# ScalarE multiplies the rows of both norms by their inverse root mean square; TensorE broadcasts the first modulation rows; the orders of work laid anew

## What is computed

```python
mod = (silu(c) @ wmod).reshape(8, 6, 1, 128)
sa, ca, ga, sb, cb, gb = mod[:, 0], ..., mod[:, 5]      # ga, gb: kept at least 0.25 away from 0
h = layernorm(x) * (1 + ca) + sa
x = x + ga * attn(h)       # h * rsqrt(mean(h*h) + eps) * w; in_proj; causal conv; silu;
                           # softplus; state-space recurrence of 4 heads; gate by silu(z); out_proj;
                           # and h itself is added as the residual
h = layernorm(x) * (1 + cb) + sb
x = x + gb * ffn(h)        # soft MoE: h / |h| * sqrt(128) * gamma; logits against 512 normed slots;
                           # softmax over tokens and over slots; 8 experts; combine
```

## Time and profile before

| | us |
|---|---|
| median of 3 runs (256.5 to 257.06) | 257.02 |
| the profiled execution, its own time | 258.02 |
| its span, first to last instruction | 256.3 |
| busy: PE, DVE, ACT, POOL | 215.7, 150.1, 130.5, 48.3 |
| granted TensorE clock, mean | 0.993 |

### The profile page before, as it was taken

The page is one execution under the profiler, slowest core; times in us unless marked ns, Lnnn a source line. Parts: engine busy times, 40 slices in busy tenths (PEclk is TensorE's granted clock), DMA queues, the critical chain, the costliest instruction groups (busy, mean ns, idle before and its releaser), DMA issues.

```text
span 256.3 us, 3390 instructions
## 1 busy us (share of the span) xinstructions
PE 215.7 (84%) x1141; PEld 136.9 (53%) x1141; DVE 150.1 (59%) x463; ACT 130.5 (51%) x270; POOL 48.3 (19%) x91
## 2 busy tenths in 40 slices
PE   3611998799778977989899789987999999998895
PEld 0311555655545756637566548674444445454894
DVE  2786788599889998679698786561020110102353
ACT  2444239964055676559932247556827254360460
POOL 5126920001462477000001640000000000000000
PEclk9999999999999999999999889999999999999999
DMA  7360000020032000000410000000033230500022
GB/s 197 79 205 1 1 0 0 12 76 0 5 128 77 0 3 0 4 0 0 132 39 0 0 1 3 0 3 0 0 82 82 51 113 0 164 4 0 20 64 82
DMA packets 13488, 10.42 MB, mean 41 GB/s; under 512 B 1582, under 2 KB 11287, under 8 KB 13471
## 3 DMA queue, kind: packets, MB, share of 16 engines
q1 hardware_dynamic: 10982, 9.02, 11.8%
q10 hardware_dynamic: 2488, 1.19, 1.9%
HBM read 9.08 MB, written 1.07 MB: 40 GB/s over the span
## 4 chain that ended last, share of the span: by engine, by line
PE 54%; DVE 25%; ACT 8%; POOL 4%; issue 4%; DMA 3%; ACTq 2%; DVEq 0%; POOLq 0%
PE bank L511 49%; DVE xcT L1205 3%; DVE cmax L1303 2%; DVE rmax L1294 2%; POOL root L463 2%; DVE bst L1054 2%; DVE hh L1136 2%; DMA rsm<-ksm 2%; ACT xcT L905 2%; DMA out_dram<-xin 1%; DVE BT L1318 1%; DVE hh L1128 1%; DVE xntok L1159 1%; PE bank L808 1%; PE bank L759 1%
## 5 line engine op out<-in xcount | busy, mean ns | idle before, releaser
L1340 DVE SCALAR_TENSOR_TENSOR seg_e<-bank,vecT,gbT 128x512 f32<-128x512 f32 x8 | 6.0, 751 | 54.1 <-PE bank L511 54.1
L511 PE MATMUL bank<-slotsT,w_sb 128*128 128x512 f32 x64 | 28.2, 593 | 0.8 <-issue 0.8
L511 PE MATMUL bank<-eo,xhT 128*128 128x129 f32 (+1 forms) x192 | 24.1, 283 | 4.4 <-DVE xhT L1277 3.3
L511 PE MATMUL bank<-xnT,winT 128*128 128x512 f32 x48 | 25.7, 666 | 1.7 <-ACT BT L908 1.7
L511 PEld LDWEIGHTS bank<-eo,xhT 128*128 128x128 f32 x192 | 22.8, 195 | 5.9 <-DVE xhT L1277 3.7
L995 ACT ACTIVATE zsT<-bank,vecT 128x512 f32<-128x512 f32 x16 | 11.0, 688 | 21.0 <-PE bank L511 20.9
L511 PEld LDWEIGHTS bank<-slotsT,w_sb 128*128 128x128 f32 x64 | 12.1, 190 | 15.9 <-issue 14.1
L463 POOL TENSOR_TENSOR root<-root,neg_half 128x2 f32<-128x2 f32 (+1 forms) x24 | 20.1, 837 | 2.0
L458 POOL TENSOR_SCALAR root<-mv 128x2 f32<-128x2 f32 (+1 forms) x12 | 4.1, 346 | 86.2 <-DVE mv L1057 81.8
L1205 DVE SCALAR_TENSOR_TENSOR xcT<-bank,convw,xcT 128x510 f32<-128x510 f32 (+2 forms) x24 | 17.7, 738 | 4.2 <-ACT xcT L905 4.2
L1268 DVE TENSOR_TENSOR seg_m<-seg_e,gm 128x512 f32<-128x512 f32 x24 | 15.5, 686 | 5.6 <-ACT seg_e L945 5.6
(11 more groups left out here) (164 smaller groups left out, 401.9 us busy)
## 6 DMA issues: line engine op xcount, KB each, us to landing
w_sb<-in_L_ffn_w_dram SPq DMA_DIRECT2D x16, 256.0 KB, 3.0
mods_bc<-mod_dram SPq DMA_DIRECT2D x8, 320.0 KB, 3.9
xin<-in_L_attn_x_dram SPq DMA_DIRECT2D x4, 256.0 KB, 3.6
out_dram<-xin SPq DMA_DIRECT2D x8, 128.0 KB, 1.8
eo<-in_L_wmod_dram ACTq DMA_DIRECT2D x1, 384.0 KB, 3.4
eo<-in_L_attn_in_proj_w_dram ACTq DMA_DIRECT2D x1, 384.0 KB
eo<-n_L_ffn_slot_embeds_dram ACTq DMA_DIRECT2D x1, 256.0 KB, 3.4
eo<-n_L_attn_out_proj_w_dram ACTq DMA_DIRECT2D x1, 128.0 KB
```

Of the source, the lines that this page charges most:

```text
L511: return nc.tensor.matmul(o, lhsT, rhs, start=start, stop=stop)
L1340: V.scalar_tensor_tensor(eoT[:, :, j, :], bank[4 + j][:, :].rearrange("p (b s) -> p b s", b=B), vecT[:, bass.ds(it * 2 + (RB2 + j), 1)], g ...
```

## The change

- `unit1` and `unit2` become visits of ACT: an Identity activation with the root as a scale of its own for each partition, in place of DVE's multiplication. Sixteen tiles for each of the two norms in all.
- The shift and scale rows of sublayer one of the first pass no longer go through HBM. PE multiplies `cs` of one batch, broadcast over 128 columns, by the first 256 columns of `wmod`, so that a PSUM bank has the rows on all partitions, and adds the 1 with a matmul of ones. `centre1` and `modulate1` of pass 0 read the bank (`mod_of`). The other rows go through HBM as before, later; `mods_bc` of pass 0 is loaded without its first two rows. POOL's `add_basis` now waits for them. The 1 is added to all scales on PE.
- Of `wmod`, ACT loads 256 columns first, SP the rest later. Input weights, small vectors and the row `dt_nat` are loaded by SP, in the order c, x of unit 0, input weights, x of unit 1, rest of `wmod`, vectors, small ones.
- `s_ready` is gone. What was the preamble's tail becomes single visits (`once`) in the lists: on ACT `scale_win`, `unit_slots`, `small_rows`, `copy_wo`, `copy_sn` and the second `rsm_rows`, most of which DVE did before; on DVE `vectors`, `rows_of_mods`, `gate_columns`; on PE `t_wo`, `t_slot_embeds`; on POOL `slot_roots`.
- `UNIT_AT` is gone. A visit has four whole numbers, one for each unit and pass, its turn on its engine; so the two passes have orders of their own.

```diff
-        UNIT_AT = [0.0, 4.04, 91.03, 95.07]
...
-        def pipeline(eng, visits):
+        def pipeline(eng, visits, once=()):
 
-            todo = sorted((p + UNIT_AT[j + 2 * it], n, j, it) for n, (p, _) in enumerate(visits)
-                          for it in range(PASSES) for j in range(2))
+            todo = sorted([(turns[j + 2 * it], n, j, it) for n, (turns, _) in enumerate(visits)
+                           for it in range(PASSES) for j in range(2)]
+                          + [(turn, n, None, None) for n, (turn, _) in enumerate(once)])
...
-            mm(bank[5][0:B, 0:3 * P], cs[:, :], wmod_sb[:, 0:3 * P])
-            mm(bank[6][0:B, 0:3 * P], cs[:, :], wmod_sb[:, 3 * P:6 * P])
-            mm(bank[7][:, 0:B], wmod_sb[:, tile_cols(5)], cs[:, :]).then_inc(s_pe0, 1)
+            one_row = ident[:, 0:1].broadcast_to((P, P))
+            for j in range(2):
+                for bi in range(BP):
+                    b, o = j * BP + bi, bank[5 + j][:, 2 * bi * P:2 * (bi + 1) * P]
+                    mm(o, cs[:, b:b + 1].broadcast_to((P, P)), wmod_sb[:, 0:2 * P], stop=False)
+                    q = mm(o[:, P:2 * P], ones_sq[:, :], one_row, start=False)
+                q.then_inc(s_pe0, 1)
             pe.wait_ge(s_vec, N_VEC)
-            nc.tensor.transpose(bank[0][:, 0:VR], vec_nat[:, :], ident[0:VR, 0:VR])
-            pe.wait_ge(s_w, N_W)
+            nc.tensor.transpose(bank[0][:, 0:VR], vec_nat[:, :], ident[0:VR, 0:VR]).then_inc(s_pe0, 1)
+            pe.wait_ge(s_w, 16)
...
+            def unit1(j, it):
+
+                wait(act, root_done, j, it, 2)
+                for t in range(TP):
+                    q = A(xntok[j][:, t, 0:P], hh[j][:, t, :], ACT.Identity, scale=root[j][:, t:t + 1])
+                q.then_inc(xn_done[1][j], 1)
+
+            def unit2(bi):
+                def visit(j, it):
+                    wait(act, ms_root_done, j, it, bi + 1)
+                    for t in range(bi * NT, (bi + 1) * NT):
+                        q = A(xn2tok[j][:, t, 0:P], hh[j][:, t, :], ACT.Identity, scale=root[j][:, t:t + 1])
+                    q.then_inc(xn2_done[1][j], 1)
                 return visit
...
-            pipeline(act, visits)
+            pipeline(act, visits, once=[(3, scale_win), (5, unit_slots), (6, small_rows), (9, copy_wo), (12, copy_sn),
+                                        (13, lambda: rsm_rows(1).then_inc(s_act0, 1))])
...
+            def vectors():
+
+                dve.wait_ge(s_pe0, PE_VEC)
+                step0(V.tensor_copy(vecT[:, :], bank[0][:, 0:VR]))
+                assert n0[0] == DVE_VEC
+                step0(V.tensor_tensor(g_all[:, :], vecT[:, RG:RG + 1], vecT[:, RSG:RSG + 1], ALU.mult))
+                assert n0[0] == DVE_G
...
+            def mod_of(j, it, bi, m):
+
+                if it == 0 and m < 2:
+                    return bank[5 + j][:, (2 * bi + m) * P:(2 * bi + m + 1) * P]
+                return mods_bc[j][:, bi, m, :]
...
             def centre1(j, it):
-                wait(dve, mods_in, j, it)
+                if it:
+                    wait(dve, mods_in, j, it)
+                else:
+                    dve.wait_ge(s_pe0, PE_MOD[j])
                 wait(dve, var_done, j, it)
                 centre(j, it, 0, range(BP), own_norm1)
...
-            pipeline(dve, visits)
+            pipeline(dve, visits, once=[(0, vectors), (7, rows_of_mods), (8, gate_columns)])
```

One line of the new numbers, of ACT's list (unit1 and unit2, for j, it = 0,0; 1,0; 0,1; 1,1):

```diff
+                      ((64, 66, 122, 123), exps(1)), ((68, 74, 124, 125), copy_slotsT(1)), ((2, 10, 65, 69), unit1),
+                      ((44, 48, 103, 108), unit2(0)), ((46, 52, 106, 112), unit2(1))]
```

More of the change, by code:

```diff
@@ L529, in _ @@
[L529 to L536 removed]
+            pe.wait_ge(s_wo, N_WO)
+            nc.tensor.transpose(bank[2][:, 2 * P:2 * P + H], dt_nat[:, :], ident[0:H, 0:H]).then_inc(s_pe0, 1)
@@ new lines, in _, with t_wo @@
+            pe.wait_ge(s_wmod_b, 16)
+            mm(bank[7][0:B, 0:3 * P], cs[:, :], wmod_sb[:, 0:3 * P], stop=False)
+            mm(bank[7][0:B, P:2 * P], ones_sq[:, 0:B], one_row, start=False)
+            mm(bank[4][0:B, 0:3 * P], cs[:, :], wmod_sb[:, 3 * P:6 * P], stop=False)
+            mm(bank[4][0:B, P:2 * P], ones_sq[:, 0:B], one_row, start=False)
+            mm(bank[7][:, 3 * P:3 * P + B], wmod_sb[:, tile_cols(5)], cs[:, :]).then_inc(s_pe0, 1)
+            def t_wo():
+                pe.wait_ge(s_dve0, DVE_ROWS)
+                for k in range(CT):
+                    q = nc.tensor.transpose(bank[7][:, tile_cols(k)], wo_nat[:, tile_cols(k)], ident[:, :])
+                q.then_inc(s_pe0, 1)
@@ L538, in _, with t_slot_embeds @@
+            def t_slot_embeds():
+                pe.wait_ge(s_act0, ACT_SE_UNIT)
+                for m in range(MT):
+                    q = nc.tensor.transpose(bank[4][:, tile_cols(m)], se_nat[:, m, :], ident[:, :])
+                q.then_inc(s_pe0, 1)
             pe.wait_ge(s_pool, POOL_ALL)
-            pe.wait_ge(s_ready, 3)
             def t_xn(j, it):
@@ L862, in _, with scale_win, unit_slots, copy_wo @@
                 act.wait_ge(s_act0, ACT_TANH + m + 1)
-            act.wait_ge(s_small, N_SMALL)
-            A(expA_t[:, :], expA_row[:, :], ACT.Exp).then_inc(s_act0, 1)
-            act.wait_ge(s_pool, POOL_ALL)
-            for j in range(2):
-                A(rsm[j][:, :, :], blk[:, 1, :].unsqueeze(2).broadcast_to((P, H, W)), ACT.Copy).then_inc(s_act0, 1)
-            act.wait_ge(s_ready, 1)
+            def scale_win():
+                act.wait_ge(s_dve0, DVE_VEC)
+                act.wait_ge(s_pe0, PE_W)
+                w = vecT[:, RNW:RNW + 1]
+                A(winT[:, 0:512], bank[1][:, :], ACT.Identity, scale=w).then_inc(s_act0, 1)
+                A(winT[:, 512:ROWS], bank[2][:, 0:ROWS - 512], ACT.Identity, scale=w).then_inc(s_act0, 1)
+            def unit_slots():
+                act.wait_ge(s_pool, POOL_SE)
+                for m in range(MT):
+                    q = A(se_nat[:, m, :], se_nat[:, m, :], ACT.Identity, scale=se_r[:, m:m + 1])
+                q.then_inc(s_act0, 1)
+            def copy_wo():
+                act.wait_ge(s_pe0, PE_WO)
+                A(woT[:, :, :], bank[7][:, 0:CT * P].rearrange("p (k d) -> p k d", k=CT), ACT.Copy).then_inc(s_act0, 1)
+            def copy_sn():
+                act.wait_ge(s_dve0, DVE_G)
+                act.wait_ge(s_pe0, PE_SE)
+                A(snT[:, :], bank[4][:, :], ACT.Identity, scale=g_all[:, :]).then_inc(s_act0, 1)
+            def small_rows():
+                act.wait_ge(s_small, N_SMALL)
+                A(expA_t[:, :], expA_row[:, :], ACT.Exp)
+                for k in range(CT):
+                    A(diag_d[:, k, :], ident[:, :], ACT.Identity, scale=d_col[:, k:k + 1])
             def mods(j, it, bi):
@@ L1151, in visit @@
                     wait(dve, var_root_done, j, it, bi + 1)
-                    modulation(j, 1, [bi]).then_inc(h2_done[1][j], 1)
-                return visit
-            def unit1(j, it):
-                wait(dve, root_done, j, it, 2)
-                for t in range(TP):
-                    q = V.tensor_scalar(xntok[j][:, t, 0:P], hh[j][:, t, :], root[j][:, t:t + 1], None, ALU.mult)
-                q.then_inc(xn_done[1][j], 1)
-            def unit2(bi):
-                def visit(j, it):
-                    wait(dve, ms_root_done, j, it, bi + 1)
-                    for t in range(bi * NT, (bi + 1) * NT):
-                        q = V.tensor_scalar(xn2tok[j][:, t, 0:P], hh[j][:, t, :], root[j][:, t:t + 1], None, ALU.mult)
-                    q.then_inc(xn2_done[1][j], 1)
+                    modulation(j, it, 1, [bi]).then_inc(h2_done[1][j], 1)
                 return visit
```

218 lines of the change are left out of this document (111 added, 107 removed).

## The result

| | before | changed |
|---|---|---|
| median (lowest to highest), 20 runs each | 258.71 (256.24 to 261.33) | 259.58 (258.77 to 261.88) |
| ratio, 95% interval | | 1.0058 (1.003 to 1.0086) |
| the profiled execution, its span | 258.02, 256.3 | 261.88, 259.9 |
| granted TensorE clock in it | 0.993 | 0.933 |

The change is slower by 0.6% by the ratio, about 1.5 us (0.9 us by the medians), where 1.7 us less than before were forecast. The 20 runs of the kernel before have a higher median than the three shown ahead of the prediction (257.02 us).

The account below looks back on a forecast made before the run. It took a thin chain to bound the head, then PE, DVE and ACT in turns, DVE in the hand-over, PE in the experts. Terms summed to -1.7 us, forecasting 255.3 us; own range 253.9 to 256.6, whole range 250.9 to 258.2 us.

Parts of the forecast that it names:

- The sum: Whole kernel: five terms, -3.0 + 1.1 - 0.2 + 0.1 + 0.3, give -1.7 us, span 256.3 to 254.6 us.
- The head: Up to the first projection: mods' broadcast by PE starts it earlier, by 2.6 to 3.6 us, taken as 3.0 us.
- ACT while the first projections run: First pass: work moved to ACT exceeds its idle time before unit 1's exponential, costing 1.1 us.
- The hand-over: First to second pass: `token_max` 1.4 us later through ACT's queue, offset by DVE's relief; 0.2 us gained.
- The table loads: Second-pass projections: two more loads of 1.28 us each and the silu nearly fit ACT's idle time; 0.1 us lost.
- The end of the second pass: ACT's queue holds `copy_logits(0)` back about 2.0 us, PE's new order gives it back; 0.3 us lost.
- the second rival: ACT's queue: waits for POOL's roots cost 1.4 and 2.0 us, nothing gives them back; +1.6 us, 258.6 us, chance 0.13.
- The first rival: DVE's relief in hand-over and second norms counts in full, 4.5 us; about 250.7 us, chance 0.22.
- the third rival: The head does not come early: vectors' loads land 2.6 us behind PE and hold every norm; 257.9 us, chance 0.14.
- fourth rivals: The fourth: second-pass table loads meet no idle time on ACT, 3.1 us more; 258.4 us, chance 0.06.

Follow-up runs that it names:

- b: Changed kernel with `unit2` moved back to DVE and `unit1` left on ACT; median 257.09 us, ratio to before 0.9889.
- d: Changed kernel with ACT's copies of xn2T and logits ahead of waiting `unit2` visits, one PE pair swapped; median 257.04 us, ratio to before 0.995.
- h: Changed kernel with unit 0's second-pass silu later on ACT, so two table loads go; median 259.48 us, ratio to before 1.0062.
- i: Changed kernel with SP issuing the six vector loads ahead of projection weights and x of unit 1; median 258.5 us, ratio to before 1.0052.
- c: Changed kernel with DVE's `vectors` moved behind the centring of both units; median 254.94 us, ratio to before 0.9898.
- k: f plus ACT's second `rsm_rows` directly behind the first and `copy_sn` ahead of unit 1's `copy_xnT`; median 251.35 us, ratio to before 0.9774.
- g: Changed kernel with the edits of c and d together; median 252.92 us, ratio to before 0.979.
- e: Changed kernel with `unit1` and `unit2` both moved back to DVE; median 258.35 us, ratio to before 1.0016.
- f: Changed kernel with the edits of b and c together; median 252.27 us, ratio to before 0.9753.
- j: f with PE's broadcast undone, the first pass's mods going through memory again; median 263.09 us, ratio to before 1.0236.
- l: k plus DVE's `unit2(1)` of unit 1 in the first pass one turn earlier; median 251.5 us, ratio to before 0.9786.
- a: Kernel before with only `unit1` and `unit2` moved from DVE to ACT; median 263.0 us, ratio to before 1.0175.

## Why the prediction was wrong

**"The sum": -1.7 us forecast, +1.5 us measured.** The terms in turn.

- **The head, -3.0 us: right as a number, for the changed kernel as built.** Four kernels have its head: b, d, h and i begin P 3.1 to 3.5 us before 25.94 us. The profiled execution itself, with -1.6 us, had the vectors land later. "DVE's `vectors` ahead of the first statistics" was seen, and put down as giving away part of the gain. It was not priced: c shows 4.7 us.
- **ACT while the first projections run, +1.1 us: right as a number, and partly by luck.** P to Y grew by 0.9 to 1.9 us in b, d, h and i, 2.35 us in the profiled execution. ACT was indeed without idle time before unit 1's exponential in b, d and i, at 35.8 to 36.1 us for the 36.2 us forecast. But PE's idle time in P to Y grew by only 0.5 us (2.2 to 2.6 us) in these four. The other 0.4 to 1.4 us are PE at work: four transposes of the slot embeddings that stand there now (0.60 us at 31.01 us in the changed kernel, 0.60 us in h, 1.06 us in i), and pace (the twelve 512-column instructions of unit 1 took 5.49 us in i and 7.19 us in h). In k ACT was idle for 3.11 us before that exponential, and P to Y was 28.77 us all the same, against 28.63 us in c.
- **"The hand-over", -0.2 us: the step that failed.** Y to P' grew by 1.3 us in the profiled execution and by 1.8 us in c, h and i. The text had "1.4 us later" for `token_max`, from ACT's queue, and then let the order and DVE's relief give it all back. Two things were wrong. The delay began at `copy_xn2T`, one step earlier than at `copy_logits`: `unit2(1)` of unit 0 was ahead of that copy in the order, and only unit 1's `unit2` was looked at. So PE stood idle 2.2 us before the logits of c, h and i, for 0.47 us before, and L is 1.9 us later. And the giving back was counted in waits alone. As waits it came: over the whole stretch PE is idle 0.5 to 1.0 us less than before. But its work took 2.2 to 2.5 us longer, of which the first four logits, behind that wait, are 1.7 to 1.8 us (3.63 to 3.78 us for 1.98 us). In the head the prediction priced PE's pace; here it put it at nothing, without a reason. How much of the lower pace the wait brings is not settled: b and d, with 0.47 us of idle time there, had it in this place too, g didn't.
- **The table loads, +0.1 us: right** in that they are hidden (h). P' to Y' is 0.5 us longer, and h does not shorten it; in c, d, e, f, g, i, j and l it is 25.9 to 26.2 us. All of these eight have a granted clock of 0.93 in this stretch; before, changed, a, b, h and k have 1.00.
- **The end of the second pass, +0.3 us: too small, for the same reason.** Y' to X is 50.58 us against 49.71 us in the profiled executions, 0.9 us more, though 49.5 to 49.9 us in c, h and i. The kernel before had a low spell of its own there, a granted clock of 0.94 in Y' to L', and this hid most of the loss. Against b, with the clock at 1.00, the queue costs 1.66 us in Y' to L', and Y' to X is 1.5 to 2.6 us longer. PE's idle time over Y' to X is nearly the same in all kernels of the second table, 5.9 to 6.5 us, so that the order gave the wait back, as was forecast; what is left is the pace behind the wait:

```profile
150.88 3.78 PE L537 MATMUL bank<-snT,CTr 128*128 128x512 f32 x4 [2.23 <-ACT CTr L987]
```

So the second rival, ACT's queue waiting for POOL's roots, came in: 0.13 was its chance, +1.6 us its price, +1.5 us the result. Its condition was stated and held: PE's first `shifts(1)` of the second pass came 64.83 us behind P' before and 65.83 us after. That its number fits so well is luck in part. It had nothing give the waits back, and they were given back; what it priced at 1.4 and 2.0 us is, in c, h and i, 1.8 us in Y to P' and between -0.2 and +0.2 us in Y' to X against the profiled execution before, and what there is of it is pace. The first rival, DVE's relief in full, is half true: for the first norm it pays 0.5 to 1.3% (e against b), for the second it does not, since ready copies stand behind it on ACT. The prediction's own sign for the second rival was the stretch from P' to X longer by over 1 us; it is 75.84 us against 74.48 us. And the third rival named the right row of the queue, `vectors`, for the wrong size, since it asked when the load lands and not what stood behind it.

Three figures of the prediction don't come out. The lower end of the forecast's own range, 253.9 us, is 253.3 us by its three conditions (257.02 - 3.6 - 0.2 + 0.1). The whole range ends at 250.9 us and so leaves the first rival's 250.7 us outside. And "slower 0.17" is less than the second and fourth rivals, both slower than before, have together (0.19).

## What to carry to other kernels

When work goes to an idle engine, look at what it waits for and what stands behind it in that queue: 0.69 us of multiplication made the first logits of a pass 1.9 and 1.7 us late, because a copy that was ready stood behind it, and the same work in the first norm paid. Price what the wait does to PE's pace as well: a later stage can give the wait back and not the pace. When a latency is taken away (here the mods' way through memory), ask of each engine's first instruction whether it is the next latency; here moving one visit gave 4.6 us. And a share of the chain that falls from 25% to 5% on one engine doesn't say that the kernel is faster: PE's rose from 54% to 65%.
